# Cross-attention scores from the turned queries directly, recurrent scores on 32x64 pieces

## The chip, the cores and the metric

One core of a Trainium2 chip (trn2). The metric is device time in microseconds (us) for the whole program. TensorE (PE) multiplies; VectorE (DVE), ScalarE (ACT) and GpSimd (POOL) do elementwise work; SyncE (SP) issues every transfer. All engines share the on-chip memory (SBUF); PE writes to eight accumulation banks (PSUM).

## The reference, cut to what matters

A decoder layer for 32 sequences of 128 tokens, width 512, float32, in three residual blocks:

```python
x = x + recurrent(layernorm(x))      # 32 heads of 16
x = x + cross(layernorm(x), ctx)     # 32 query heads, 8 key/value heads of 16
x = x + ffn(layernorm(x))            # 512 -> 2048 -> 512, operands rounded in blocks of 32

# recurrent: r, k, v, g are projections of x mixed with its predecessor in time
att = rr @ kk * Wm                   # Wm: decay w^(t-s-1) for s < t, bonus u at s = t
y = att @ vv + rr @ state * wb       # chunks of 64 in the reference
# cross: 4 query heads share a key/value head; keys and values are both ctx
scores = einsum('bkgsd,bktd->bkgst', qh, kh) / sqrt(16)
out = einsum('bkgst,bktd->bkgsd', softmax(scores), vh)
```

Kernels here compute the recurrence for all 128 tokens at once, with a 128x128 decay table per head.

## The kernel before, in words

The 32 sequences are independent. Each engine has a block of code with small functions, one per step, with the sequence `n` as argument, and then a written-out list of calls: its program order. Semaphores named after the producer tie the engines. Lists for the first and last sequences are written out; the middle is a loop over `n` (10 to 28) with one period's calls, in which steps of up to five sequences are interleaved. Each engine works strictly through its list, so the place of a step in the list decides what waits behind it. SP has such a list too, and a transfer that waits for its source holds up all behind it.

On PE a period consists of, in this order before the change: `turn_x` (L496, transposes of the normalised x), `values_r` half 0 (L554), `turn_out` (L623), `scores_max` half 1 (L590), `project g`, `scores_max` half 0, `project r`, `scores_r` half 1 (L534), `turn_maxima` (L600), `project k`, `values_r` 1, `scores_x` 0 (L605), `head_variance` (L571), `project_v` (L515), `values_x` 0 (L612), `scores_x` 1, `up` 1 and 0 (L629), `project_out` (L578), `values_x` 1, `scores_r` 0, `down` 0 and 1 (L639), `turn_queries` (L584), `turn_sums` (L619), `up` 2 and 3. The four banks `rt` (one per row group g of the array) are shared by both kinds of scores and by the turned queries; `bank_o` holds transposes and outputs, `bank_a` and `bank_b` projections, `bank_y` the sums over values and `down`.

**Recurrent scores.** `scores_r(n, i)` does two of four blocks m of 128 channels. Row group g holds 32 channels, two heads of 16. The score of one head alone is had by setting the other head's 16 channels to 0 in one operand: POOL writes `rz` (late half of the receptances, two parities, L2947) and `kz` (early half of the keys, L2944) as products with a mask. Per m and g one matmul has all 128 keys against the late receptances of both parities (128 columns, L546) and one has the early keys of both parities against the early receptances (64 columns, L550). DVE multiplies with the decay table `wm` (`decayed`, L1451). `values_r` multiplies with the values: `vz` holds them spread with zeros, `vp` the early half of both parities stacked in partitions, which SP copies in two transfers (`earlier_values`, L216).

**Cross attention.** ACT writes the normalised x with the query heads reordered (`normalise_x`), PE turns it, ACT copies it as `qdense` (`queries_x`, L2396): 8 key/value heads x 16 channels in the partitions, then 4 query heads j and 128 tokens. `queries_spread` (L225) moves 16 partitions at a time so that each head of half i starts a 32-partition row group in `qx`: 4 transfers per half, 8 per sequence. `scores_max` (L590) computes the scores a first time, from `qx` and the turned context `kx`, 4 j x 4 g matmuls of 128 columns on 16 rows per half; DVE reduces them to the negated row maxima (`maxima`, L1484), PE turns these, ACT copies them, and `maxima_to_rows` (L245) puts them as a 17th row into `qx`. `scores_x` (L605) computes the scores a second time, transposed and with the maximum subtracted, 4 matmuls of 512 columns per half. ACT takes the exponential (`weights_x`), PE multiplies with the context (`values_x`), whose extra column of ones yields the sums. ACT copies the result (`out_x`, L2418), `outputs_gathered` (L235) moves the sums (1 transfer per half) and outputs (4 per half) to the dense layout for the turn back. DVE divides (`normalise_o`).

**Feed-forward.** `up` and `down` read bf16 operands that are rounded by chains on DVE (`hidden_*`, `gelu_*`) with one scaling per gelu half on POOL (`gelu_scale`, L2971), and turned by SP transfers (`hidden_turned` L259, `gelu_turned` L266). `first_sum` (DVE, L1477) follows `project_out`; the statistics of the next x and `normalise_q` (ACT) lead to `turn_x`.

## Time and profile before

| | us |
|---|---|
| median of 3 runs (lowest, highest) | 1427.66 (1426.7, 1431.09) |
| the profiled execution's own time | 1427.9 |
| its span in the profile | 1426.1 |
| PE busy (share), matmul records | 1285.7 (90%), 13352 |
| DVE busy (share) | 1137.4 (80%) |
| ACT busy (share) | 806.6 (57%) |
| POOL busy (share) | 657.5 (46%) |
| mean granted TensorE clock | 0.951 |

A float32 matmul appears as two records in the profile, so 16 matmuls are x32. In the timeline a group's length runs to the modelled end of its last matmul, which overlaps the next group; the time that a group takes from the engine is the distance of two starts. "Idle before" is the time the engine stood idle ahead of the group, with what ended it. The clock is given as a share of 2.4 GHz.

### The profile page before, as it was taken

To read this page: it belongs to the slowest core of one execution; us is meant where nothing else is said; L and a number is where in the kernel's file an instruction comes from. 1 tells how busy PE (TensorE), PEld (TensorE's weight loads), DVE (VectorE), ACT (ScalarE), POOL (GpSimd) and SP (SyncE) were. 2 spreads that over 40 slices of the span, in tenths; PEclk is the share of its full clock that TensorE was granted. 3 is DMA by queue.
4 is the path that set the end of the run, shared out by engine and by line. 5 is a ranking of instruction groups with operands and counts; after the bars stand their busy time and mean duration, and the time that the engine had idled before them with its cause. 6 is when DMAs were issued, how large, how long until landed. Compare 5 with 4: busy or idle time off the path is not lost.

```text
span 1426.1 us, 34930 instructions
## 1 busy us (share of the span) xinstructions
PE 1285.7 (90%) x13352; PEld 835.6 (59%) x13352; DVE 1137.4 (80%) x1960; ACT 806.6 (57%) x1541; POOL 657.5 (46%) x668
## 2 busy tenths in 40 slices
PE   2868789999999999999999999999999999999754
PEld 1745566556666665656666666656666666665321
DVE  5879778777878878888888878888887887877675
ACT  2233365656666656666666656656666665665441
POOL 3655445343545444544555454444455544543222
PEclk8878899999999999999999999999999999999776
DMA  9245313222212222222212222222221222222122
GB/s 307 56 121 126 71 41 60 64 58 52 61 45 59 56 61 57 66 64 52 62 46 57 54 66 57 66 64 63 54 62 42 63 54 64 57 66 57 36 49 48
DMA packets 143989, 95.04 MB, mean 67 GB/s; under 512 B 113744, under 2 KB 115792, under 8 KB 143056
## 3 DMA queue, kind: packets, MB, share of 16 engines
q1 hardware_dynamic: 143824, 92.80, 26.6%
q8 instruction: 108, 1.77, 0.5%
q14 instruction: 57, 0.47, 0.1%
HBM read 32.97 MB, written 8.39 MB: 29 GB/s over the span
## 4 chain that ended last, share of the span: by engine, by line
PE 74%; DVE 7%; DMA 6%; SPq 5%; issue 4%; ACT 2%; POOL 1%; POOLq 0%; DVEq 0%; ACTq 0%
PE bank_b L530 15%; PE bank_a L530 8%; PE bank_y L644 8%; PE bank_y L581 7%; PE bank_a L520 7%; PE rt L596 5%; PE rt L609 5%; PE bank_o L615 4%; DMA qx<-qdense 4%; SPq L233 3%; PE rt L546 3%; PE bank_o L575 2%; PE bank_b L635 2%; PE bank_a L635 2%; PE rt L550 1%
## 5 line engine op out<-in xcount | busy, mean ns | idle before, releaser
L2974 POOL TENSOR_TENSOR gmem<-gmem,unit_g 128x1024 bf16<-128x1024 bf16 x64 | 132.1, 2064 | 242.2 <-DVE unit_g L1540 242.2
L1488 DVE TENSOR_REDUCE negm<-rt 128x16 f32<-128x2048 f32 x64 | 146.4, 2287 | 44.2 <-PE rt L596 44.1
L2415 ACT ACTIVATE pT<-rt 128x2048 f32<-128x2048 f32 x64 | 120.1, 1877 | 45.2 <-PE rt L609 41.1
L644 PE MATMUL bank_y<-w2q,gmem 128*128 128x512 bf16 x512 | 123.4, 394 | 20.3 <-DMA gmem<-gmem 20.2
L530 PE MATMUL bank_b<-mix_k,w_Wk 128*128 128x128 f32 x1024 | 123.6, 280 | 15.4 <-DVE mix_k L1435 15.4
L530 PEld LDWEIGHTS bank_b<-mix_k,w_Wk 128*128 128x128 f32 x1024 | 121.9, 198 | 17.5 <-DVE mix_k L1435 12.8
L530 PE MATMUL bank_b<-mix_g,w_Wg 128*128 128x128 f32 x1024 | 130.8, 289 | 0.0
L530 PEld LDWEIGHTS bank_b<-mix_g,w_Wg 128*128 128x128 f32 x1024 | 125.1, 203 | 4.3 <-issue 0.7
L530 PE MATMUL bank_a<-mix_r,w_Wr 128*128 128x128 f32 x1024 | 126.7, 283 | 0.0
L530 PEld LDWEIGHTS bank_a<-mix_r,w_Wr 128*128 128x128 f32 x1024 | 120.7, 197 | 3.9 <-issue 0.4
L581 PE MATMUL bank_y<-w_Wo,yT 128*128 128x512 f32 x256 | 118.6, 607 | 3.6 <-DVE yT L1475 3.6
L2965 POOL TENSOR_TENSOR gt<-gt,yT 128x512 f32<-128x512 f32 x32 | 43.6, 1362 | 166.1 <-ACT yT L2394 166.0
L520 PE MATMUL bank_a<-w_Wv,mix_v 128*128 128x512 f32 x256 | 115.4, 593 | 3.3 <-ACT rT L2341 2.6
L1459 DVE TENSOR_TENSOR att<-rt,wm 128x1536 f32<-128x1536 f32 x64 | 112.0, 1749 | 4.9 <-PE rt L550 4.6
L2377 ACT ACTIVATE gh<-bank_b,all_columns 128x128 f32<-128x128 f32 x128 | 36.5, 369 | 126.5 <-PE bank_b L530 126.5
L596 PE MATMUL rt<-context,qx 16*128 16x128 f32 x2048 | 80.8, 297 | 28.0 <-DMA qx<-qdense 19.4
L644 PEld LDWEIGHTS bank_y<-w2q,gmem 128*128 128x128 bf16 x512 | 48.7, 100 | 82.2 <-issue 27.2
L596 PEld LDWEIGHTS rt<-context,qx 16*128 16x128 f32 x2048 | 68.9, 199 | 39.4 <-issue 27.3
L2958 POOL TENSOR_TENSOR gh<-gt,half_ln 128x512 f32<-128x512 f32 x32 | 53.9, 1684 | 77.6 <-DVE gt L1466 77.6
L520 PEld LDWEIGHTS bank_a<-w_Wv,mix_v 128*128 128x128 f32 x256 | 48.4, 190 | 64.2 <-issue 61.3
L2979 POOL TENSOR_TENSOR x<-x,o_bf 128x512 f32<-128x512 f32 x32 | 37.3, 1165 | 102.1 <-DVE o_bf L1607 102.1
L581 PEld LDWEIGHTS bank_y<-w_Wo,yT 128*128 128x128 f32 x256 | 49.2, 194 | 60.0 <-issue 56.3
(192 smaller groups left out, 2916.6 us busy)
## 6 DMA issues: line engine op xcount, KB each, us to landing
xin<-x SPq DMA_DIRECT2D x32, 256.0 KB, 3.0
gmem<-w SPq DMA_DIRECT2D x16, 512.0 KB, 4.0
vp<-vz SPq DMA_DIRECT2D x64, 128.0 KB, 2.9
context<-ctx SPq DMA_DIRECT2D x32, 256.0 KB, 2.7
qx<-qdense SPq DMA_DIRECT2D x256, 32.0 KB, 2.0
odense<-oT SPq DMA_DIRECT2D x256, 32.0 KB, 2.0
out<-x SPq DMA_DIRECT2D x32, 256.0 KB, 2.3
w_Wg<-Wg SPq DMA_DIRECT2D x1, 1024.0 KB, 7.6
```

What stands on the lines that cost most here:

```text
L520: done = e.matmul(bank_a[:, :], mix["v"][:, c, :], wt["Wv"][:, c, :], start=(c == 0), stop=(c == KT - 1))
L530: done = e.matmul(bank[:, m * T:(m + 1) * T], wt[f"W{name}"][:, c, m * P:(m + 1) * P], mix[name][:, c, :], start=(c == 0), stop=(c == KT - 1))
L581: done = e.matmul(bank_y[:, :], yT[:, c, :], wt["Wo"][:, c, :], start=(c == 0), stop=(c == KT - 1))
L596: done = e.matmul(rtb(g)[:, j * T:(j + 1) * T], qx[rows16, i, j, :], kx[n % 2][rows16, i, :], start=True, stop=True)
L609: done = e.matmul(rtb(g), kx[n % 2][rows32, i, :], qx[rows32, i, :, :], start=True, stop=True)
L615: done = e.matmul(bank_o[32 * g:32 * g + 32, :], kv[n % 2][:, 4 * i + g, :], pT[:, g, :], start=True, stop=True)
L635: done = e.matmul(bank[:, :], hqT[:, c, :], w1q[:, 4 * j:4 * j + 4, c, :], start=(c == 0), stop=(c == KT - 1))
L644: done = e.matmul(bank_y[:, :], gqT[:, t, :], w2q[:, t, :], start=(t == 0), stop=(t == FT - 1))
L1459: e.tensor_tensor(att[:, :, :, :, :].rearrange("p g m k t -> p g (m k t)"), rt[:, :].rearrange("p (g n) -> p g n", g=4)[:, :, 0:6 * HALF], ...
L1488: e.tensor_reduce(negm[:, 0:H].rearrange("p (g i j) -> p g i j", g=4, i=2)[:, :, i, :], rt[:, :].rearrange("p (g j s) -> p g j s", g=4, j= ...
L2415: e.activation(pT[:, :, :].rearrange("p g n -> p (g n)"), rt[:, :], ACT.Exp, scale=float(D) ** -0.5).then_inc(sem(f"act_ex{i}"), 1)
L2974: e.tensor_tensor(blocks(half), blocks(half), per_block(unit[f"g{i}"], 32), ALU.mult).then_inc(sem(f"pool_gsc{i}"), 1)
```

## The change

What it does:

- The turned context comes in a second form, `kd`: keys of two neighbouring heads in one row group, 256 columns, each with the other head's 16 rows at 0. `scores_max` multiplies `qdense` with it directly; half i now means query heads 2i and 2i+1 instead of key/value heads 4i to 4i+3. It waits for the ACT copy, no longer for a transfer.
- `queries_spread` is one step with two transfers of 112 partitions; `scores_x` and what follows take even key/value heads as half 0, odd ones as half 1. The even outputs are already in their place: ACT writes them to `odense`; the odd ones go through `oT` and four transfers.
- `kz` is gone. `rz` has four parts of 64 columns: early and late receptances of the first parity, late and early of the second. `scores_r` issues three matmuls per m and g (192, 128 and 64 columns) whose stationary side has 64 columns, two of them writing partitions 64 to 127.
- POOL fills `rz` in one step with three tensor_scalars. ACT copies the first parity of `vp`; one transfer is left.
- The order of the calls is new on all engines. The loop now covers n = 10 to 26.

Functions:

```diff
-ODD = 2 * H * D // 2 + D
+ODD = H * D + D
             def load_ctx(n):
...
+                        e.wait_ge(sem(f"pe_Xs{i}"), n - 1)
...
-            def queries_spread(n, i):
+            def queries_spread(n):
                 e.wait_ge(sem("act_qdense"), n + 1)
                 if n:
-                    e.wait_ge(sem(f"pe_Xt{i}"), n)
+                    e.wait_ge(sem("pe_Xt0"), n)
+                    e.wait_ge(sem("pe_Xt1"), n)
...
-                for g in range(4):
-                    kvh = 4 * i + g
-                    e.dma_start(qx[32 * g:32 * g + D, i, :, :], qdense[D * kvh:D * kvh + D, :, :])...
+                for i in range(2):
+                    e.dma_start(qx[0:P - D, i, :, :], qdense[D * i:P - D + D * i, :, :])...
+            def odd_outputs(n):
+                e.wait_ge(sem("act_oT1"), n + 1)
+                sums_gathered(n, 1, oT)
+                e.wait_ge(sem("sp_oden0"), 16 * (n + 1))
                 for g in range(4):
-                    kvh = 4 * i + g
-                    e.dma_start(odense[D * kvh:D * kvh + D, :, :], oT[32 * g:32 * g + D, i, :, :])...
+                    e.dma_start(odense[32 * g + D:32 * g + 32, :, :], oT[32 * g:32 * g + D, :, :])...
             def maxima_to_rows(n):
                 e.wait_ge(sem("act_neg"), n + 1)
+                e.wait_ge(sem("sp_qx"), 32 * (n + 1))
...
             def scores_r(n, i):
...
-                    for g in range(4):
-                        e.matmul(rtb(g)[:, mm * 3 * HALF:(mm * 3 + 2) * HALF], kT[rows32, m, :], rz[rows32, m, :, :], ...)
-                    for g in range(4):
-                        done = e.matmul(rtb(g)[:, (mm * 3 + 2) * HALF:(mm * 3 + 3) * HALF], kz[rows32, m, :, :],
-                                        rT[rows32, m, 0:HALF], ...)
+                pieces = ((0, 0, 0, 3), (1, 1, 1, 3), (1, 0, 3, 4))
+                    for side, keys, q0, q1 in pieces:
+                        for g in range(4):
+                            at = (3 * mm + q0 % 3) * HALF
+                            done = e.matmul(rtb(g)[HALF * side:HALF * side + HALF, at:at + (q1 - q0) * HALF],
+                                            kT[rows32, m, HALF * keys:HALF * keys + HALF], rz[rows32, m, q0:q1, :], ...)
             def scores_max(n, i):
                 e.wait_ge(sem(f"sp_ctx{n % 2}"), 16 * (n // 2 + 1))
-                e.wait_ge(sem(f"sp_qx{i}"), 64 * (n + 1))
-                for j in range(GQ):
+                e.wait_ge(sem("act_qdense"), n + 1)
+                for jj in range(2):
                     for g in range(4):
-                        done = e.matmul(rtb(g)[:, j * T:(j + 1) * T], qx[rows16, i, j, :], kx[n % 2][rows16, i, :], ...)
+                        done = e.matmul(rtb(g)[:, jj * 2 * T:(jj + 1) * 2 * T], qdense[rows32, 2 * i + jj, :],
+                                        kd[n % 2][rows32, :, :], ...)
...
+            def values_copied(n):
...
+                e.activation(vp[0:HALF, :, :], vz[0:HALF, 0:H * D].rearrange("p (q c) -> p q c", q=PAIRS), ACT.Copy)...
...
-            def earlier_keys(n):
-                of_parity(n, "pool_kz", kz, kT[:, :, 0:HALF], "act_kT")
-            def later_receptances(n):
-                of_parity(n, "pool_rz", rz, rT[:, :, HALF:T], "act_rT")
+            def by_parity(n):
+                e.wait_ge(sem("act_rT"), n + 1)
...
+                e.tensor_scalar(rz[:, :, 0:2, :], rT[:, :, :].rearrange("p k (e t) -> p k e t", e=2), parity[:, 0:1], 1.0, ...)
+                e.tensor_scalar(rz[:, :, 2, :], rT[:, :, HALF:T], parity[:, 1:2], 1.0, ALU.mult, ALU.mult)
+                e.tensor_scalar(rz[:, :, 3, :], rT[:, :, 0:HALF], parity[:, 1:2], 1.0, ...)
```

The orders of a period after the change, where they matter (each list goes round):

- PE: `head_variance`, `project_v`, `values_x` 0, `scores_x` 1, `up` 1, `up` 0, `project_out`, `scores_r` 0, `values_x` 1, `up` 2, `down` 0, `down` 1, `turn_queries`, `up` 3, `turn_sums`, `values_r` 0, `turn_x`, `scores_max` 1, `turn_out`, `project g`, `scores_max` 0, `project r`, `scores_r` 1, `turn_maxima`, `project k`, `values_r` 1, `scores_x` 0.
- ACT: ... `out_even`, `values_copied`, `weights_x` 1, two `gelu`, `out_odd`, `normalise_x`, `normalise_q`, `queries_x`, `x_turned`, `gate_tanh`, `gate_in`, two `gelu`, `maxima_turned`, `normalise_f`, `receptance`, `squares`. Before, `queries_x` came right ahead of `rstd_log q` and `normalise_q`.
- DVE: `norm_mv f` comes behind the second `maxima` and `mixed k` instead of ahead of them; `gelu_pow2` behind `gated_y`.
- POOL: `gate_rstd`, `by_parity`, `gelu_scale` 1, `gelu_scale` 0, `with_bias`, `last_sum`, `mixed r`, `second_sum`, `mixed g`, `gate_parts`. Before, `later_receptances` came ahead of `gate_rstd` and `earlier_keys` behind it.
- SP: `hidden_turned`, `even_sums`, `gelu_turned` 0, `earlier_values`, `gelu_turned` 1, `next_x`, `odd_outputs`, `load_ctx`, `queries_spread`, `store`, `maxima_to_rows`.
- At the start `Wv` is loaded ahead of the feed-forward weights, the third piece of these is loaded ahead of the first transposing transfer, and `project r` comes ahead of `project k` for sequence 0. At the end `up` of sequence 31 comes ahead of `down` half 1 of sequence 30, and on DVE the hidden state of 31 ahead of the last gelu half of 30.

## Rows read from the trace of the kernel before

**Rows 1.** The page, part 2: granted TensorE clock in the 40 slices.
```profile
PEclk8878899999999999999999999999999999999776
```

**Rows 2.** The page, part 4: the chain that ended last, by line.
```profile
PE bank_b L530 15%; PE bank_a L530 8%; PE bank_y L644 8%; PE bank_y L581 7%; PE bank_a L520 7%; PE rt L596 5%; PE rt L609 5%; PE bank_o L615 4%; DMA qx<-qdense 4%; SPq L233 3%; PE rt L546 3%; PE bank_o L575 2%; PE bank_b L635 2%; PE bank_a L635 2%; PE rt L550 1%
```

**Rows 3.** Stretches: us, busy (x) of PE, PEld, DVE, ACT, POOL, clock, DMA, GB/s.
```profile
251.20:1330.30 1079.10, 1041.80 (x11161) 678.16 (x11157) 877.38 (x1550) 672.79 (x1286) 511.59 (x529) 0.99 0.24 58
```

**Rows 4.** Waits of PE, 251.2 to 1330.3 us: total us, times, longest.
```profile
PE rt L596 <- DMA qx<-qdense: 15.2, 17, 2.0
PE bank_o L499 <- ACT xx L2316: 12.7, 26, 1.3
PE rt L596 <- DVE negm L1488: 3.4, 3, 1.8
```

**Rows 5.** Timeline of PE: start us, us, what, [idle before <-releaser].
```profile
974.80 1.12 PE L575 MATMUL bank_o<-yT,masks 128*128 128x512 f32 x2
...
1012.71 1.14 PE L609 MATMUL rt<-qx,context 32*128 32x512 f32 x8
1013.78 1.12 PE L575 MATMUL bank_o<-yT,masks 128*128 128x512 f32 x2
```

**Rows 6.** Timeline of PE in the same period, from project_out's end.
```profile
986.62 1.07 PE L615 MATMUL bank_o<-pT,context 128*32 128x512 f32 x8
987.62 0.50 PE L546 MATMUL rt<-rz,kT 32*128 32x128 f32 x8
...
988.67 3.63 PE L644 MATMUL bank_y<-w2q,gmem 128*128 128x512 bf16 x16
...
995.16 0.63 PE L499 MATMUL bank_o<-masks,xx 128*128 128x128 f32 x4 [0.42 <-ACT xx L2316]
995.72 0.32 PE L562 MATMUL bank_y<-att,vp 128*32 128x64 f32 x8
...
996.53 0.65 PE L626 MATMUL bank_o<-masks,odense 128*128 128x128 f32 x4
997.28 1.17 PE L596 MATMUL rt<-context,qx 16*128 16x128 f32 x32
998.38 3.84 PE L530 MATMUL bank_b<-mix_g,w_Wg 128*128 128x128 f32 x32
```

**Rows 7.** Timeline of PE at 517 us, and the stretch 518 to 524 us.
```profile
517.13 1.77 PE L596 MATMUL rt<-context,qx 16*128 16x128 f32 x32 [1.67 <-DMA qx<-qdense]
518.84 6.46 PE L530 MATMUL bank_b<-mix_g,w_Wg 128*128 128x128 f32 x32
...
518.00:524.00 6.00, 6.00 (x43) 5.78 (x37) 3.62 (x5) 0.00 (x0) 2.69 (x3) 0.50 0.05 11
```

**Rows 8.** Timelines of ACT and of SP's queue in that period.
```profile
992.77 0.60 ACT L2401 ACTIVATE qdense<-rt 128x512 f32<-128x512 f32 x1 [1.31 <-PE rt L587]
...
993.39 2.40 SPq L233 DMA_DIRECT2D qx<-qdense  x4
```

**Rows 9.** Timelines of POOL, at the start and in that period, and of DVE.
```profile
42.67 3.02 POOL L2924 TENSOR_SCALAR mix_g<-xx,all_columns 128x128 f32<-128x128 f32 x4
...
979.48 1.04 POOL L2939 TENSOR_TENSOR kz<-kT,masks 128x512 f32<-128x512 f32 x1
981.19 2.27 POOL L2974 TENSOR_TENSOR gmem<-gmem,unit_g 128x1024 bf16<-128x1024 bf16 x1 [0.68 <-DVE unit_g L1540]
...
983.90 0.41 DVE L1587 TENSOR_SCALAR gmem<-gmem 128x1024 f16<-128x1024 bf16 x1
...
986.73 0.69 DVE L1482 TENSOR_TENSOR x<-bank_y,xin 128x512 f32<-128x512 f32 x1 [0.55 <-PE bank_y L581]
```

**Rows 10.** SP's queue, PE's first up, and the median landing from the issues by line.
```profile
978.42 1.26 SPq L264 DMA_TRANSPOSE hqT<-hz  x1
...
981.36 1.04 PE L635 MATMUL bank_b<-w1q,hqT 128*128 128x512 bf16 x4
...
hqT<-hz SPq DMA_TRANSPOSE x32, 2.5
```

More of the change, by code:

```diff
@@ new lines, in _ @@
+            e.wait_ge(sem("act_expv"), 51)
+            values_x(24, 0)
+            e.wait_ge(sem("act_ex0"), 25)
+            scores_x(24, 1)
+            e.wait_ge(sem("act_kT"), 27)
+            up(23, 1, bank_b)
+            e.wait_ge(sem("dve_vz"), 27)
+            up(23, 0, bank_a)
+            e.wait_ge(sem("dve_yz"), 26)
+            project_out(25)
+            e.wait_ge(sem("act_ex1"), 25)
+            scores_r(26, 0)
+            e.wait_ge(sem("act_oT0"), 25)
+            values_x(24, 1)
@@ new lines, in _ @@
+            scores_x(25, 1)
+            e.wait_ge(sem("act_kT"), 28)
+            up(24, 1, bank_b)
+            e.wait_ge(sem("dve_vz"), 28)
+            up(24, 0, bank_a)
+            e.wait_ge(sem("dve_yz"), 27)
+            project_out(26)
+            e.wait_ge(sem("act_oT0"), 26)
+            values_x(25, 1)
+            e.wait_ge(sem("act_ex1"), 26)
+            scores_r(27, 0)
+            e.wait_ge(sem("dve_ze0"), 25)
+            up(24, 2, bank_a)
+            e.wait_ge(sem("dve_x1"), 27)
@@ new lines, in _ @@
+                gelu_quantised(n - 4, 0)
+                decayed(n - 1, 1)
+                stats_g(n - 3)
+                norm_mv("g", n - 3)
+                mixed(n, "v")
+                weighted(n - 3)
+            hidden(23)
+            hidden_max(23)
+            hidden_pow2(23)
+            hidden_scale(23)
+            hidden_round(23)
+            hidden_quantised(23)
+            gelu_max(22, 1)
+            scaled_y(25)
+            spread_v(26)
+            gated_y(25)
+            gelu_pow2(22, 1)
@@ new lines, in _ @@
+            up_out(23, 1, bank_b)
+            up_out(23, 0, bank_a)
+            gelu_round(22, 1)
+            gelu_quantised(22, 1)
+            first_sum(25)
+            stats_x(25)
+            norm_mv("x", 25)
+            gelu_max(23, 0)
+            gelu_pow2(23, 0)
+            decayed(26, 0)
+            stats_q(27)
+            norm_mv("q", 27)
+            second_out(22)
+            residual(22)
+            denominators(24)
+            up_out(23, 2, bank_a)
+            up_out(23, 3, bank_b)
@@ new lines, in _ @@
+            gelu_round(23, 0)
+            differences(27)
+            maxima(25, 1)
+            normalise_o(24)
+            stats_f(24)
+            maxima(25, 0)
+            norm_mv("f", 24)
+            mixed(27, "k")
+            gate(26)
+            gelu_quantised(23, 0)
+            decayed(26, 1)
+            stats_g(24)
+            norm_mv("g", 24)
+            mixed(27, "v")
+            weighted(24)
+            hidden(24)
+            hidden_max(24)
+            hidden_pow2(24)
@@ L3226 @@
     pairs = np.arange(H).reshape(2, 2, 4, 2).transpose(0, 2, 1, 3).reshape(PAIRS, 2)
[L3227 removed]
+    order = np.stack([np.concatenate([pairs[:, a:a + 1], pairs], 1).reshape(3 * PAIRS) for a in range(2)])
     heads = np.concatenate([get("L0_attn_time_decay")[order], get("L0_attn_time_faaaa")[order]], 1)
```

1744 lines of the change are left out of this document (983 added, 761 removed).

## The prediction

> **What bounds the kernel now.** I read the slices of the page first, then the chain, then three stretches, then one period. In the slices [rows 1] the granted TensorE clock is full (9 of 10 or more) from the sixth slice to the last few. In the chain that ended last [rows 2] every costly entry is a PE line, with two exceptions that belong together: the transfer of the queries (4%) and its issue on SP's queue (3%). So TensorE's instruction order is the path, and the spread of the queries is the one thing outside it that the path passes through often. The stretches [rows 3] cut the run where it changes character: 251.2 us of start, 1079.1 us in the middle, 95.7 us of end. The middle begins and ends with the same instruction (the head variance) 27 sequences apart, so a period is 1079.1/27 = 39.97 us. PE is busy 1041.8 of it: 37.3 us are idle, and three rows hold 31.3 of them [rows 4]: 15.2 for the queries' transfer, 12.7 for the normalised x, 3.4 for the row maxima. A period without trouble takes 1013.78 - 974.80 = 38.98 us [rows 5]. Beside the idle time there is a hidden loss: behind a wait of 1.67 us for the queries, the projection of g took 6.46 us instead of 3.84 and the clock stood at 0.50, the 1.2 GHz level, for 6 us [rows 6, 7]. Four such drops stand in the middle, each right behind such a wait; the others are shorter, and I count 2.1 us each, 8.5 us. DVE (877.4 of 1079.1) is the next engine, with 19% to spare.
>
> **Queries.** Today scores_max waits until four transfers per half have landed: the copy of the turned queries takes 0.60 us, the issue of one half 2.40 us, and then the landing follows [rows 8]. After the change it waits for the ScalarE copy alone. The 15.2 us and the 8.5 us of clock go. The new transfers (two of 112 rows, then the maxima) are needed only by scores_x, more than 10 us later, so their size (by the code 0.46 MB for the pair against 0.26) costs nothing unless they hold up the maxima behind them, for whose transfer PE waits nowhere in the middle today [rows 4]. SP issues 16 instead of 27 transfers a period. Outputs: the even half is copied straight into its place; four transfers instead of eight, none of which PE waited for in the middle. Gain 0, cover kept. The context load grows by half and is issued over one period ahead.
>
> **What is late next.** In ScalarE's order the copy of the queries moves behind normalise_q, which shortens the chain to turn_x by about 0.5 us (0.60 less overlap); on PE the first values_r (996.53 - 995.72 = 0.81 us) moves ahead of turn_x. From the end of project_out (986.62) to turn_x (995.16) are 8.54 us, of which 0.42 is the wait [rows 6]. The chain behind it then needs 8.0, while PE has 8.9 us of work: the wait goes, 12.7 us. The copy of the queries then ends about 0.6 us before PE asks for it. The maxima: scores_max for half 1 moves ahead of turn_out (997.28 - 996.53 = 0.75 us more for the reduction), so 3.4 us go too.
>
> **First scores.** Before, each half was 16 matmuls of 128 columns on 16 rows, 998.38 - 997.28 = 1.10 us. After, 8 of 256 columns on 32 rows. Per row group both stream 512 columns; scores_x, 4 matmuls of 512, takes 1013.78 - 1012.71 = 1.07 [rows 5, 6]. Bounds 1.07 and 1.20 (were the wider load exposed); I take 1.07, saving 0.06 per period.
>
> **Recurrent scores.** Before: 988.67 - 987.62 = 1.05 us per half for 384 columns per row group [rows 6]. After: 12 matmuls per m, in two column halves of the array with 192 columns each, loads of 64 instead of 128 columns. scores_x and values_r (384 columns in 0.81) both run at 2.1 ns per column. If the halves run side by side, that is 384 x 2.1 = 0.81 us; if they take turns, 768 x 2.1 = 1.61. The nearest row is values_r, many short matmuls on parts of the array that do overlap, but there no piece follows another on the same row group with other columns. I take 1.00, a fifth over the floor: 0.05 saved twice, 0.10 per period. The first range end saves 0.48, the last costs 1.12.
> The Trainium skill (TensorE: Matmul & The Clock Gate, Part 3, "The mechanism") says that weight loads overlap running matmuls only when the row group differs. By it the loads of the second column half would wait for the first half's streams, which is the second rival below. Its page TensorEngine Tiling (Array Packing), "Key Properties", says that different tiles load and multiply in parallel, which is the low end. No row of the kernel before has two column pieces in one row group, so the trace does not decide.
>
> **Other engines.** POOL: two products of 512 elements, 1.04 us each [rows 9], become three tensor_scalars with 1024 elements in all. Two products' worth is 2.1 us; eight of the 128-column tensor_scalars are 6.0 us at the worst row (four in 3.02, beside DVE, at the start). I take 2.5. What queues behind it is the scale of the gelu half (starts 981.19, 2.27 us), for which DVE's rounding waits (starts 983.90). It would start about 982.0 and end 984.3: DVE's rounding 0.4 us late, inside the 0.55 us that DVE idles before first_sum. Cost 0. ACT gets the copy of the first values: 64 rows of 512 at most the 0.60 us of the queries' copy; it stands ahead of weights_x(1), whose result is not needed for 3 us. ACT is busy 672.8 of 1079.1. Cost 0. DVE: norm_mv f moves behind the maxima, 0.3 us onto the chain to the turned hidden states. That transfer is issued at 978.42, lands 2.5 us later at 980.9, and up begins at 981.36 [rows 10]: 0.4 us of slack, of which 0.3 go by this and 0.05 by faster scores. I leave 0.1 us per period for it and for the transfers whose issue now and then takes a microsecond longer.
>
> **The sum.** Middle, per period: 39.97 - 0.56 (queries) - 0.31 (clock) - 0.47 (turn_x) - 0.13 (maxima) - 0.16 (scores) + 0.10 = 38.44, so -1.53, times 27 = -41 us. Start, 6 sequences: the same, less because other waits set their end, -1.0 each, -6. There Wv is also loaded earlier, and the third piece of W1 before the transposes; I count nothing for it but 8 us in the range. End, 2 sequences: -3, and hidden(31) now runs ahead of the last gelu half, -2. Together -52. The profiled execution took 1427.9 us (span 1426.1), 0.2 over the median of 1427.66, so the two need no correction: 1427.7 - 52 = 1375.5; I say 1375.
>
> **The rivals.**
> 1. *A new wait keeps the period near the untroubled one.* The chain through DVE (maxima, mixing, gate, decayed scores, hidden states, transposing transfer) has 0.4 us of slack and gets longer while PE gets shorter. For it: DVE would be at 33/38.4. Against: in the period of [rows 5] PE waits for nothing but x. It would hold 39.1 us: gain 0.87 x 27 = 23, plus 11: 1393.
> 2. *The column halves take turns*, or the loads are exposed: 1.61 instead of 1.00 per half, +1.2 us per period in all 32, +38: 1413. For: the scores of today, 1.05 against a floor of 0.81, already show loads [rows 6]; against: values_r at its floor.
> 3. *Slower.* POOL's parity step is the mechanism. Its output is ready far ahead of scores_r, but the gelu scale queues behind it, and behind that DVE's rounding, first_sum, the statistics, turn_x. The chain has 0.5 us (DVE's idle time) and 0.9 us (PE's slack at turn_x). At 2.5 us nothing happens; each microsecond over about 3.5 is one per period; from about 5.4 us on, the 52 us are lost. At the 6.0 us of the worst row: 2.5 x 27 = 67 lost, 1442. For: [rows 9], 3.02 for four. Against: in the same place today nothing contends, 1.04 for 512.
> 4. *The change takes nothing off the path*: another transfer of that place in SP's queue (the outputs, the maxima) inherits the long issue and lands just as late for PE. Then only scores and turn_x gain, 0.5 x 32 = 16 from the 52 remain, 1412; with the scores at their high bound, no change at all. Against: in the middle PE waited for none of them once.
>
> **Numbers.** Chances: forecast 0.60, first rival 0.14, second 0.11, fourth with some gain 0.05, no change 0.03, slower 0.07. All pieces at their floor (-0.38 x 32 = -12), the start 8 better and the end 4 better give 1351 at the low end; at the high end the range takes in rivals 1, 2 and 4: 1413. A difference under 0.3% (4 us) could not be told from none. Faster 0.90, same 0.03, slower 0.07.
>
> **What would show it.** Right: no wait of PE for the queries' transfer; full clock in the middle; head variances 38.2 to 38.7 us apart; scores_r 0.9 to 1.1 us per half; turn_x without its 0.42. Wrong: a wait of up for hqT in each period (rival 1); recurrent scores near 1.6 us (2); a parity step over 3.5 us and DVE waiting for the gelu scale (3); PE waiting for odense or the maxima's row (4).

## The result and the profile after

The changed kernel takes 1364.58 us (median of 4 runs, 1364.28 to 1369.35), the kernel before in the same comparison 1429.38 us (1426.7 to 1432.94). The ratio is 0.9553, with a 95% interval of 0.9521 to 0.9585: about 64 us faster, where 52 were forecast. The profiled span is 1362.5 us. In the chain of the changed kernel TensorE's share is 80%, and DMA's is 3% over all its transfers; before, the queries' transfer and its issue alone held 7% [rows 2].

The page of the changed kernel, parts 1 and 2 (busy time with its share and instructions; granted TensorE clock in 40 slices):

```profile
PE 1254.7 (92%) x13352; PEld 801.5 (59%) x13352; DVE 1137.3 (83%) x1960; ACT 823.8 (60%) x1577; POOL 631.8 (46%) x700
...
PEclk8878899999999999999999999999999999999876
```

The same three stretches as before, cut at the same two head variances (us, then busy time and instructions of PE, PEld, DVE, ACT, POOL, then clock, DMA share, GB/s):

```profile
0.00:247.50 247.50, 180.56 (x1964) 128.41 (x1964) 198.93 (x302) 107.31 (x216) 119.69 (x129) 0.89 0.41 113
247.50:1275.60 1028.10, 1022.12 (x11168) 654.54 (x11164) 879.37 (x1553) 682.43 (x1314) 488.92 (x557) 1.00 0.26 63
1275.60:1362.50 86.90, 52.00 (x229) 18.56 (x225) 58.99 (x108) 34.03 (x47) 23.17 (x14) 0.76 0.22 50
```

Against [rows 3] the middle lost 1079.1 - 1028.1 = 51.0 us, the start 251.2 - 247.5 = 3.7, the end 95.8 - 86.9 = 8.9. In the middle TensorE is idle for 6.0 us where it was idle for 37.3, and its clock is 1.00 where it was 0.99. The waits over 0.2 us that are left there (total us, times, longest) come once each; neither the queries' transfer nor the normalised x of [rows 4] is among them:

```profile
PE rt L566 <- DVE negm L1614: 1.6, 1, 1.6
PE bank_y L580 <- DVE att L1585: 1.6, 1, 1.6
PE bank_o L516 <- DVE x L1630: 1.5, 1, 1.5
PE bank_b L654 <- DMA hqT<-hz: 0.8, 1, 0.8
```

The periods are 38.04 us in all but a few of the 27, and in such a period TensorE waits for nothing. This is the one that answers to [rows 5, 6], on PE's timeline:

```profile
973.89 1.12 PE L593 MATMUL bank_o<-yT,masks 128*128 128x512 f32 x2
...
985.71 1.14 PE L566 MATMUL rt<-rz,kT 32*64 32x192 f32 x48
986.78 1.07 PE L633 MATMUL bank_o<-pT,context 128*32 128x512 f32 x8
...
993.50 0.24 PE L640 MATMUL bank_o<-masks,oden 32*128 32x32 f32 x1
993.67 0.32 PE L580 MATMUL bank_y<-att,vp 128*32 128x64 f32 x8
...
994.48 0.66 PE L516 MATMUL bank_o<-masks,xx 128*128 128x128 f32 x4
995.07 1.15 PE L614 MATMUL rt<-context,qdense 32*128 32x256 f32 x16
996.14 0.66 PE L645 MATMUL bank_o<-masks,odense 128*128 128x128 f32 x4
996.63 3.74 PE L547 MATMUL bank_b<-mix_g,w_Wg 128*128 128x128 f32 x32
...
1011.93 0.70 PE L593 MATMUL bank_o<-yT,masks 128*128 128x512 f32 x1
```

Read it from start to start, since the printed durations overlap. The first scores take 996.14 - 995.07 = 1.07 us. The recurrent scores take 986.78 - 985.71 = 1.07, where they took 1.05: the pieces of 32x64 gave nothing. The turning of the outputs takes 0.49 us, where it took 0.75 [rows 6], of which TensorE idled for 0.09. The input is turned at 994.48 with no wait.

POOL's parity step in that period:

```profile
978.47 0.69 POOL L3251 TENSOR_SCALAR rz<-rT,masks 128x512 f32<-128x512 f32 x1
979.13 0.48 POOL L3253 TENSOR_SCALAR rz<-rT,masks 128x256 f32<-128x256 f32 x1
979.58 0.48 POOL L3254 TENSOR_SCALAR rz<-rT,masks 128x256 f32<-128x256 f32 x1
981.09 1.90 POOL L3282 TENSOR_TENSOR gmem<-gmem,unit_g 128x1024 bf16<-128x1024 bf16 x1 [1.02 <-DVE unit_g L1667]
```

SP's queue, the issue of the hidden states' transfer:

```profile
976.89 1.23 SPq L273 DMA_TRANSPOSE hqT<-hz  x1
```

The parity step takes 1.6 us (2.5 forecast), and POOL then waits 1.02 us for DVE. `up` starts at 980.45, 3.56 us after that issue, which leaves 1.1 us over the 2.5 of [rows 10]; the forecast had counted on 0.1.

### The profile page after: what moved, and what is told of

The parts are those of the page before. It is cut to its first block, busy times and chain, and to the rows that moved or that the text cites. A ratio compares the mean times of both kernels' runs of the same rounds, so it can differ in the third digit from the quotient of the medians.

```text
span 1362.5 us, 34643 instructions
## 1 busy us (share of the span) xinstructions
PE 1254.7 (92%) x13352; PEld 801.5 (59%) x13352; DVE 1137.3 (83%) x1960; ACT 823.8 (60%) x1577; POOL 631.8 (46%) x700
## 4 chain that ended last, share of the span: by engine, by line
PE 80%; DVE 8%; issue 5%; DMA 3%; POOL 2%; ACT 2%; POOLq 0%; SPq 0%; DVEq 0%; ACTq 0%
PE bank_b L547 15%; PE bank_a L547 8%; PE bank_y L599 8%; PE bank_y L663 7%; PE bank_a L537 7%; PE rt L614 5%; PE rt L566 4%; PE rt L627 4%; PE bank_o L633 4%; PE bank_b L654 4%; PE bank_a L654 4%; PE bank_o L593 2%; PE bank_y L585 2%; PE bank_y L580 1%; DMA gmem<-w 1%
## 5 line engine op out<-in xcount | busy, mean ns | idle before, releaser
L3282 POOL TENSOR_TENSOR gmem<-gmem,unit_g 128x1024 bf16<-128x1024 bf16 x64 | 124.5, 1945 | 239.1 <-DVE unit_g L1667 239.1
L2626 ACT ACTIVATE pT<-rt 128x2048 f32<-128x2048 f32 x64 | 120.1, 1876 | 20.2 <-PE rt L627 19.4
L547 PE MATMUL bank_b<-mix_g,w_Wg 128*128 128x128 f32 x1024 | 120.6, 276 | 0.0
L547 PEld LDWEIGHTS bank_b<-mix_g,w_Wg 128*128 128x128 f32 x1024 | 117.2, 192 | 1.6 <-issue 1.3
L2578 ACT ACTIVATE gt<-bank_b,half_bg 128x128 f32<-128x128 f32 x128 | 36.6, 370 | 83.3 <-PE bank_b L547 83.3
L566 PEld LDWEIGHTS rt<-rz,kT 32*64 32x64 f32 x3072 | 63.1, 131 | 33.3 <-issue 24.0
L1655 DVE TENSOR_REDUCE amax_g<-gmem 128x32 f32<-128x1024 bf16 x64 | 77.8, 1215 | 1.7 <-ACT gmem L2658 1.6
L1719 DVE SCALAR_TENSOR_TENSOR gmem<-gmem,pow_g 128x1024 bf16<-128x1024 f16 x64 | 78.2, 1222 | 1.1
```

The lines of the kernel that those rows point to most:

```text
L547: done = e.matmul(bank[:, m * T:(m + 1) * T], wt[f"W{name}"][:, c, m * P:(m + 1) * P], mix[name][:, c, :], start=(c == 0), stop=(c == KT - 1))
L566: done = e.matmul(rtb(g)[HALF * side:HALF * side + HALF, at:at + (q1 - q0) * HALF], kT[rows32, m, HALF * keys:HALF * keys + HALF], rz[rows ...
L1655: e.tensor_reduce(amax[key][:, :], blocks(src), AX_X, ALU.max, apply_absolute_value=True).then_inc(sem(name), 1)
L1719: e.scalar_tensor_tensor(blocks(half), blocks(half.bitcast(FP16)), MAGIC16, per_block(pow2[f"g{i}"], 32), ALU.subtract, ALU.mult).then_inc ...
L2626: e.activation(pT[:, :, :].rearrange("p g n -> p (g n)"), rt[:, :], ACT.Exp, scale=float(D) ** -0.5).then_inc(sem(f"act_ex{i}"), 1)
L3282: e.tensor_tensor(blocks(half), blocks(half), per_block(unit[f"g{i}"], 32), ALU.mult).then_inc(sem(f"pool_gsc{i}"), 1)
```

## Experiments

Times "in place of" are against the changed kernel's 1364.58 us and ratio of 0.9553. "The middle" is always from the fifth to the last head variance, 27 periods.

**1. The old recurrent scores in the changed kernel.**

```
-  pieces = ((0, 0, 0, 3), (1, 1, 1, 3), (1, 0, 3, 4))
+  e.matmul(rtb(g)[:, (mm * 3 + 1) * HALF:(mm * 3 + 3) * HALF], kT[rows32, m, :], rz[rows32, m, :, :],
+           start=True, stop=True)
+  e.matmul(rtb(g)[:, mm * 3 * HALF:(mm * 3 + 1) * HALF], kz[rows32, m, :, :], rT[rows32, m, 0:HALF],
+           start=True, stop=True)
```

> The changed kernel with the recurrent scores of the kernel before (a 128-column and a 64-column matmul for each head on 32x128 pieces, the keys' parity product back on POOL); order of the work and cross attention as changed. Theory: the 32x64 pieces gave nothing (scores_r takes 1.07 us in the changed kernel, 1.05 before), so 1364 us, 1360 to 1368. Rival, as forecast: the pieces save 0.05 us per half, two halves in 32 batches, so 3 us slower, 1368. Second rival: the 0.41 us per period of the middle that no wait explains came from the pieces, so 27 x 0.41 = 11 us slower, 1376.

Measured: 1364.99 us, ratio 0.9562 (0.9539 to 0.9585), the same. The undisturbed period is 38.00 us, 0.04 shorter than with the pieces. PE's timeline shows the half as it was before:

```profile
757.42 0.50 PE L565 MATMUL rt<-rz,kT 32*128 32x128 f32 x8
...
758.20 0.35 PE L569 MATMUL rt<-rT,kz 32*128 32x64 f32 x8
758.47 0.64 PE L635 MATMUL bank_o<-pT,context 128*32 128x512 f32 x4
```

1.05 us, from 757.42 to 758.47. By time alone the first rival's 3 us could not be told from nothing; the period can: by that rival it would be 38.14 us. So the third part of the change is worth nothing, both rivals fall, and the gain is in the other two parts.

**2. The wait for the queries' transfers put back.**

```
 def scores_max(n, i):
     e.wait_ge(sem("act_qdense"), n + 1)
+    if 8 <= n <= 24:
+        e.wait_ge(sem("sp_qx"), 32 * (n + 1))
```

> The changed kernel in which the first scores of batches 8 to 24 also wait for the two transfers of queries that they no longer read. Theory: these transfers were the bound. They are issued at 994.10 in the traced period, take 2.13 us of issuing and some 3.1 to land, so they are back at about 998.3, and the first scores, which start at 995.07, lose 3.2 us in each of 17 periods: 55 us, and some 5 more for clock drops, so 1420 us (1405 to 1435); TensorE's waits on qx come back. Rival: other work slides into the gap (the first scores' place was not what bound), under 10 us, 1374 at most.

Measured: 1448.12 us, ratio 1.0128 (1.0089 to 1.0167): 84 us more than the changed kernel, and 0.9 to 1.7% more than the kernel before, above the range that was given. PE's waits, 400 to 1200 us; then one of them on PE's timeline; then the stretch behind it:

```profile
PE rt L616 <- DMA qx<-qdense: 52.3, 17, 3.6
```

```profile
725.86 2.09 PE L616 MATMUL rt<-context,qdense 32*128 32x256 f32 x16 [3.10 <-DMA qx<-qdense]
727.88 1.11 PE L647 MATMUL bank_o<-masks,odense 128*128 128x128 f32 x4
728.79 5.19 PE L547 MATMUL bank_b<-mix_g,w_Wg 128*128 128x128 f32 x32
```

```profile
725.86:733.96 8.10, 8.10 (x56) 7.23 (x56) 3.58 (x3) 0.00 (x0) 2.31 (x2) 0.63 0.00 1
```

The wait came out as worked out, 52.3 us over 17 periods against 54. The clock did not: 5 us were allowed for it, and some 30 are there: the middle grew by 1112.8 - 1028.1 = 84.7 us, of which the wait is 52.3. Behind a wait of 3.10 us the granted clock is 0.63 for the next 8.1 us, and the same projection takes 5.19 us in place of 3.74. At 15 of the 17 waits the clock falls to half, during the wait or just behind it, for 71 us in all. So a wait of the first scores for this transfer is paid in full and more, and in the new order it would be worse than it was in the old one (3.1 us each, against 15.2 us in 17 waits).

**3. The new data flow alone**, in the order of the kernel before and with its recurrent scores: `scores_max` reads `qdense` against `kd`, two transfers for the queries, four for the outputs and two for the sums; SP's list has the queries as one step in place of two, and nothing else is changed.

> The kernel before with the changed data flow of cross attention alone (first scores from the turned queries against a dense copy of the keys, four transfers for queries and for outputs); its order of the work and its recurrent scores stay. Theory: the data flow takes away the wait for the queries (15.2 us of the middle) and the clock drops (8.5), and the order gave the rest, so 24 us less than 1429, 1405 (1398 to 1412). Rival A: the order was worth nothing by itself, and this kernel has nearly the whole gain, 1375 or less. Rival B: in the old order the next wait (the turned input's, 12.7 us in the middle, or the maxima's) grows by what the queries' loses, and the time is above 1418.

Measured: 1391.44 us, ratio 0.9739 (0.9714 to 0.9765). That is 36 us of the gain, 12 more than the theory gave; rivals A and B fall. The stretches (three, as above) and PE's waits in the middle:

```profile
0.00:244.80 244.80, 179.36 (x1803) 126.76 (x1804) 200.79 (x301) 102.57 (x209) 122.92 (x125) 0.90 0.44 119
244.80:1297.40 1052.60, 1024.03 (x10268) 653.05 (x10293) 876.94 (x1550) 673.17 (x1286) 512.40 (x529) 1.00 0.25 64
1297.40:1389.80 92.40, 53.67 (x229) 19.15 (x233) 61.63 (x111) 31.41 (x47) 22.73 (x14) 0.78 0.22 51
```

```profile
PE bank_o L494 <- ACT xx L2313: 12.8, 26, 1.3
PE rt L591 <- DVE negm L1484: 6.2, 8, 1.8
```

Of the 36 us, 26.5 are in the middle: the queries' 15.2, the clock's 8.5, and an undisturbed period that is 38.76 in place of 38.98 us (27 x 0.22 = 5.9), less 2.8 by which the wait for the maxima grew (26.8 together). The wait for the normalised x is what it was, 12.8 us in 26 periods. So the order of the work is what takes it away, and the order is worth the other 24.5 us of the middle (1052.6 - 1028.1). By the rows that is nearly this wait's 12.8, 4.6 of the maxima's (6.2 to 1.6), and 8.1 from shorter steps in an undisturbed period (27 x 0.30, its wait of 0.42 left out). Whether the order costs something in the start is not shown: it is 244.8 us here and 247.5 in the changed kernel, but in the nine runs whose order of the start is the changed kernel's (it and runs 1, 2, 4 to 7, 11 and 12) it lies between 244.2 and 248.8.

**4 to 6. Which step of the order.** Both moves around the turning of the input undone in the 17 periods of the loop, then each alone.

```
 # TensorE (runs 4 and 5)             # ScalarE (runs 4 and 6)
-values_r(n - 1, 0)                   +queries_x(n - 2)
 turn_x(n)                             rstd_log("q", n); rstd_exp("q", n); normalise_q(n)
+values_r(n - 1, 0)                   -queries_x(n - 2)
```

> The changed kernel in which, in the 17 periods of the loop, TensorE's turning of the next input stands ahead of the first half of the recurrent values again, and ACT's copy of the queries ahead of the logarithm for the next input. Theory: turning the input waits 0.4 us again, since the chain from project_out to it is 7.9 us long and TensorE has that much less between them, so 17 x 0.45 = 8 us slower, 1372 (1368 to 1376). Rival: the wait is made up later in the period, within 2 us of 1364.

Measured: 1386.03 us, ratio 0.9707 (0.9685 to 0.9728): 21 us more, not 8. Each of the 17 periods is 39.48 us, 1.44 over 38.04. ACT's timeline, then PE's:

```profile
776.54 0.60 ACT L2612 ACTIVATE qdense<-rt 128x512 f32<-128x512 f32 x1 [1.15 <-PE rt L605]
777.04 0.28 ACT L2510 ACTIVATE logv_q<-mv_q,eps 128x1 f32<-128x1 f32 x1
```

```profile
778.93 0.63 PE L516 MATMUL bank_o<-masks,xx 128*128 128x128 f32 x4 [1.39 <-ACT xx L2529]
```

ACT waits 1.15 us for TensorE's turned queries, with the logarithm for the next input queued behind; in the changed kernel that logarithm needed only 0.23 us of waiting for DVE. The copy's 0.5 us and the wait's 1.15, less those 0.23, are the 1.4 us by which the normalised x is later. The run isn't the old order again, in which only 0.42 us were waited: there TensorE turned the queries 17.3 us behind the head variance (992.13 - 974.80), and here as in the changed kernel 18.2 us behind it (992.11 - 973.89), since one `up` now stands ahead of it. With the copy back in its old place, the normalised x therefore comes at 21.1 us and not at 20.2 as in the kernel before.

> As the run with both orders put back, but TensorE's order alone is put back (turning the next input ahead of the first half of the recurrent values); ACT keeps the changed order. Theory from that run's trace: the 1.44 us per period came from ACT, where the copy of the queries waits 1.15 us for TensorE's turning and the logarithm for the next input stands behind it. With ACT's order as changed the normalised input is there 19.7 us into the period and the old place of the turn begins at 19.8, so nothing is lost: 1364.5 us (1362 to 1368). Rival, as forecast: TensorE's order carries the gain, 17 x 0.4 us = 7 us slower, 1371.

Measured: 1372.65 us, ratio 0.9609 (0.9580 to 0.9639), period 38.56 (+0.52). The theory said +0 and fell, but not in favour of the rival's reason either: the normalised x is there, and the turn waits for something that no text had named (7.7 us in 17 waits).

```profile
768.24 0.24 PE L640 MATMUL bank_o<-masks,oden 32*128 32x32 f32 x1
768.93 0.66 PE L516 MATMUL bank_o<-masks,xx 128*128 128x128 f32 x4 [0.45 <-DVE rden L1622]
```

The input is turned into `bank_o`, into which the sums were turned just before, and DVE must take their reciprocals out of it first. The values, which use another bank, fill that round trip.

> The other half of that run: ACT's order alone is put back (copy of the queries ahead of the logarithm), TensorE keeps the changed order. Theory: the input is ready 1.5 us later, at 21.2 us into the period, and TensorE, which comes to its turn at 20.6 with the values already done, waits 0.65 us in each of 17 periods: 11 us slower, 1375.5 (1372 to 1379); so values ahead of the turn are worth 0.8 us per period, but only with the late ACT. Rival: the whole 1.44 us stays, 1386 as in the run with both.

Measured: 1372.80 us, ratio 0.9608 (0.9583 to 0.9633), period 38.67 (+0.63), within the range of the theory; the waits for xx sum to 10.0 us in 17 periods. The three runs fit one rule: the turn starts at the last of three times, counted from the head variance. The sums' reciprocals are out of the bank at 20.3 us, the normalised x is there at 19.7 with the new order on ACT and at 21.1 with the old one, and with the values ahead TensorE itself comes at 20.6. Either move alone leaves half a microsecond, both are needed, and undoing both costs more (1.44) than the two single costs together (1.15), because the 0.81 us of values then stand behind the wait and no longer fill it.

**7. A longer parity step on POOL**, the forecast's rival on the slow side.

```
 def by_parity(n):
+    e.tensor_tensor(spare2, rT, rT, ALU.mult)
+    e.tensor_scalar(spare[:, :, 0:2, :], rT[:, :, :].rearrange("p k (e t) -> p k e t", e=2), parity[:, 0:1], 1.0, ALU.mult, ALU.mult)
+    e.tensor_scalar(spare[:, :, 2, :], rT[:, :, HALF:T], parity[:, 1:2], 1.0, ALU.mult, ALU.mult)
+    e.tensor_scalar(spare[:, :, 3, :], rT[:, :, 0:HALF], parity[:, 1:2], 1.0, ALU.mult, ALU.mult)
```

> The changed kernel in which POOL's parity step also multiplies into a spare buffer (the same three products once more, and a product of the receptance with itself), so that it takes about 4.4 us in place of 1.6. Theory from the changed kernel's trace: POOL waited 1.02 us for DVE behind this step, so the scaling of the gelu blocks starts 1.8 us later; DVE's 1.11 us of idle time ahead of the first sum takes most of it, and TensorE's 0.85 us between the normalised input and its turn the rest: nothing is lost, 1364.5 us (1362 to 1370). Rival, as in the forecast's third rival: the cover ends at 3.5 us and each us beyond costs one, 0.9 us in 32 periods, 1393 us. If the transposing transfers of the gelu, which stand behind the same scaling, have no slack, the wait shows at TensorE's down product.

Measured: 1379.28 us, ratio 0.9657 (0.9629 to 0.9686), 15 us more. From the first to the last of its instructions the step took 4.6 us (median), where it took 1.6. PE's waits in the middle:

```profile
PE bank_b L656 <- DMA hqT<-hz: 6.9, 6, 1.2
PE rt L568 <- DVE negm L1616: 4.6, 6, 1.6
PE rt L568 <- POOL rz L3261: 2.4, 2, 1.4
```

DVE's timeline, in the changed kernel and then in run 7:

```profile
985.82 0.69 DVE L1608 TENSOR_TENSOR x<-bank_y,xin 128x512 f32<-128x512 f32 x1 [1.11 <-PE bank_y L599]
```

```profile
766.34 0.43 DVE L1716 TENSOR_SCALAR gmem<-gmem 128x1024 f16<-128x1024 bf16 x1 [1.20 <-POOL gmem L3289]
```

Neither theory holds. DVE now idles ahead of the rounding, for POOL's scaling, and no longer ahead of the first sum (0.03 us there on average, where it was 1.04). That much is the forecast's chain. Its end is another: TensorE waits only 0.2 us for the normalised x in all of the middle, and instead for the row maxima and the hidden states' transfer. That these come late because everything behind the first sum slips on DVE fits the rows, but no run takes it apart. Twice TensorE waits for the parity step's own output, which the forecast had called ready far ahead. The forecast's rule (free up to 3.5 us, then one for one) gives 1.1 us per period at 4.6, and 0.57 were paid (middle 1043.5 us). If each further microsecond costs one, the cost starts near 4 us; one point can't tell that from a slower rise. At the 1.6 us that the step really takes there is none.

**8 to 10. The head of the program.** The start gained less than forecast. In the changed kernel TensorE's first projection starts at 42.34 us, because DVE's statistics of the first input stand behind the scaling of a weight block whose load lands at 31.3:

```profile
31.30 1.22 DVE L1739 TENSOR_REDUCE amax_w<-gmem 128x32 f32<-128x1024 f32 x1 [4.86 <-DMA gmem<-w]
...
32.95 0.69 DVE L1521 BATCH_NORM_STATS2 stats_q<-xin 128x6 f32<-128x512 f32 x1
```

Run 8 moves the first input ahead on DVE, ACT and POOL and loads Wr first; run 9 also moves the first values' bias, the second input's differences and the first decays ahead of weight blocks; run 10 also the first batch's gated output and the third input's load. DVE's order in run 10, in the part that changed (the statistics of the first input stand ahead of `distances`):

```
 w12_scale(0); w12_scale(1); w12_quantise(0)
+differences(0); bonus_added(0); w12_quantise(1); mixed(0, "k"); bonus_added(1); mixed(0, "v")
+stats_q(1); w12_scale(2); w12_quantise(2); spread_v(0); w12_scale(3); differences(1)
+w12_quantise(3); decayed(0, 0); w12_scale(4); mixed(1, "k"); w12_scale(5); decayed(0, 1)
+w12_quantise(4); gate(0); w12_quantise(5); w12_scale(6); scaled_y(0); gated_y(0)
```

> The changed kernel with another head: the statistics and the normalising of the first input ahead of the building of the decays, its differences and mixes ahead of the scaling of the third block of weights, and Wr loaded first among the four projection weights. Theory: TensorE's first projection starts at 42.3 us now, since DVE's statistics stand behind the scaling of a block of weights that lands at 31.3; here it starts at 27 to 30, and the start to batch 4 gets 5 to 12 us shorter: 1355 us (1352 to 1360). Rival: the scaling and turning of the feed-forward weights set the pace of the start by themselves, the lead is given back before batch 4, and the time stays within 3 us of 1364.5.

Measured: 1360.96 us, ratio 0.9534 (0.9507 to 0.9561).

> The run with the early first input, and in it also DVE's bias of the first values, the second input's differences and the first decays moved ahead of the scaling of weight blocks, with POOL's and SP's queues to match. Theory: in that run TensorE had its first three products done at 39.6 us and then waited 14.6 us for the second input, because DVE's 0.7 us of work on the first values stood behind the weight blocks until 52; here that wait is 2 to 4 us, and the start to batch 4 gets 6 to 10 us shorter, 1353 us (1349 to 1357). Rival: DVE's and POOL's total work on the sixteen blocks sets the pace, and the lead is lost at batches 1 to 3 as before: 1359 to 1362.

Measured: 1358.09 us, ratio 0.9515 (0.9489 to 0.9541).

> The run with the early values, and in it also DVE's two steps on the gated output of the first batch, the second batch's mix for the values and POOL's parity step of it moved ahead of the scaling of the sixth to eighth weight blocks; the load of the third input stands ahead of the tenth block's. Theory: in that run TensorE waited 12.2 us at the first output projection because these steps stood behind weight blocks until 73.4 us; they can be done at 66, and 4 to 7 us of it reach batch 4, 1352.5 us (1349 to 1356). Rival: the sixteen blocks set the pace, and what is won at batch 0 is waited for at batches 1 to 3, 1356 to 1360.

Measured: 1355.25 us, ratio 0.9505 (0.9488 to 0.9523). The waits on PE's timeline at the head, run 8, run 9 and run 10:

```profile
25.96 6.61 PE L547 MATMUL bank_a<-mix_r,w_Wr 128*128 128x128 f32 x32 [9.01 <-POOL mix_r L3242]
...
54.16 1.08 PE L516 MATMUL bank_o<-masks,xx 128*128 128x128 f32 x4 [14.59 <-ACT xx L2530]
```

```profile
42.62 1.00 PE L516 MATMUL bank_o<-masks,xx 128*128 128x128 f32 x4 [2.42 <-ACT xx L2530]
...
73.60 5.29 PE L599 MATMUL bank_y<-w_Wo,yT 128*128 128x512 f32 x8 [12.17 <-DVE yT L1601]
```

```profile
66.62 5.50 PE L599 MATMUL bank_y<-w_Wo,yT 128*128 128x512 f32 x8 [5.83 <-DVE yT L1601]
```

Each run removes the wait that it aims at, and most of what it wins is waited for at the next place. The first projection starts 16.4 us earlier in run 8 and the fifth head variance only 2 (245.5 against 247.5 us), which is within the 244.2 to 248.8 of the other runs; it is at 242.0 in run 9 and at 237.3 in run 10, where the first head variance is 14.6 us early (59.7 against 74.3). Part of the lead is also paid to the clock: the projection that starts at 25.96, behind 9.01 us of idling, takes 6.61 us at a mean granted clock of 0.55, where an undisturbed one takes 3.74 to 3.84 at full clock. Neither theory nor rival holds whole: the weight blocks do not set the pace by themselves, but every step that is moved ahead finds one behind it that wasn't. Only run 10 came out within the range given for it. The intervals of runs 8 and 9 overlap that of the changed kernel. Run 10 is by the ratios 0.5%, some 7 us, faster than the changed kernel, with intervals that just touch (0.9488 to 0.9523 and 0.9521 to 0.9585), so it is probably the fastest here; its middle is the same 1028.1 us, and the start is 10.2 us shorter (1.0 of it stands at the very start, where Wv lands at 8.1 in place of 9.1 us).

**11 and 12. Why the pieces gave nothing.** Run 11 leaves the scores of the first keys against the last 64 query columns out.

Its edit is the first added line, run 12's the second:

```
-pieces = ((0, 0, 0, 3), (1, 1, 1, 3), (1, 0, 3, 4))
+pieces = ((0, 0, 0, 3), (1, 1, 1, 3))
+pieces = ((0, 0, 0, 3), (1, 0, 3, 4), (1, 1, 1, 3))
```

> The changed kernel without the third of the three pieces of the recurrent scores (first keys against the last 64 query columns), which leaves out that part of the scores. Theory: the first two pieces do run side by side (in the trace the 128-column piece starts 25 ns after the 192-column one on the same rows), and the 1.07 us per half comes from the third, which stands behind the second on the same columns of the array and holds up the next four heads in TensorE's order: a half takes 0.80 to 0.90 us here, 0.2 us less, 1364.5 - 32 x 0.4 = 1352 us (1349 to 1357). Rival: the 192-column pieces or the loads set the time, a half stays at 1.00 to 1.07, and the time is within 4 us of 1364.5.

> The changed kernel with the pieces in the order 192, 64, 128 columns in place of 192, 128, 64. Theory: the short piece is done while the 192 columns stream, and the second one of its array columns follows without holding up the next heads: 0.95 to 1.02 us per half in place of 1.07, 2 to 6 us less, 1361 us (1358 to 1364). Rival: the order within a column half makes no difference, since both orders stream 192 columns there: 1.07 us, 1364.5 within 3.

Measured: run 11 1358.16 us, ratio 0.9502 (0.9479 to 0.9526), 1 us above its range, though the half takes what its theory said; run 12 1364.67 us, ratio 0.9549 (0.9531 to 0.9568), the same as the changed kernel. PE's timeline, run 11, then run 12:

```profile
756.24 0.88 PE L566 MATMUL rt<-rz,kT 32*64 32x192 f32 x32
757.05 0.64 PE L633 MATMUL bank_o<-pT,context 128*32 128x512 f32 x4
```

```profile
756.78 1.14 PE L566 MATMUL rt<-rz,kT 32*64 32x192 f32 x48
757.86 0.64 PE L633 MATMUL bank_o<-pT,context 128*32 128x512 f32 x4
```

Two pieces take 757.05 - 756.24 = 0.81 us. That is the forecast's floor for 384 columns at 2.1 ns each, with the 128-column pieces wholly hidden: one behind the other, the 640 columns of a row group would take 1.34 us at that rate (an estimate). So the two column halves do work side by side. The third piece, of 64 columns, adds 0.26 us, and it adds as much when it comes second (1.08), so the theory of run 12 (a blocked order) falls. What the third piece pays for (its loads, its place in TensorE's queue, or the change of columns) stays open; its share of the columns alone isn't it, since its half of the array then streams 192 columns like the other. Run 11 also shows what is late next. Its undisturbed period is 37.52 us, and the hidden states' transfer is waited for again:

```profile
PE bank_b L654 <- DMA hqT<-hz: 8.2, 7, 1.4
```

## Why the prediction was right, and where not

- **Direction, mechanism, range.** Right: 1364.6 lies within 1351 to 1413, 10 us under the 1375. The middle gained 51.0 us where 41 were forecast. What had been said would show it right is there: no wait for the queries' transfer, full clock in the middle, turn_x without its wait. The head variances are 38.04 us apart, below the 38.2 to 38.7 that were given.
- **Queries, 15.2 us of wait.** Right, by runs 2 and 3. The larger transfers cost nothing in the middle, where TensorE never waits for them or for the maxima behind them.
- **Clock, 8.5 us.** Right in kind: the middle's clock is 1.00, also in run 3, and run 2 brings the drops back. The 8.5 us are half of the 17 us that the clock stood at 0.50 in four drops. A fifth, from 1319.7 us on, fills the last 10.6 us of the middle before, behind a wait of 1.82 us for the row maxima; the forecast rightly kept it out, and the changed kernel has one in that place too, 4.5 us of it in the middle. The price of such drops is not a fixed addition to each wait: run 2's text allowed 5 us for them and some 30 came.
- **turn_x, 12.7 us.** Right that the wait goes, by both moves together. The chain from project_out's end to the normalised x was put at 8.0 us and is 993.59 - 985.71 = 7.9, with TensorE coming at 8.8 (8.9 forecast). The reason for the move on TensorE was incomplete: by itself it covers DVE's reciprocals (run 5).
- **Maxima, 3.4 us.** 1.6 are left, in one wait; a term of 0.13 per period was 0.07.
- **First scores.** 1.07 us, as taken.
- **Recurrent scores: the term that failed.** 1.00 us was taken per half, 1.07 came, so the 0.10 gained per period was 0.04 lost (run 1). The halves do overlap, which the range's low end had supposed and the rule of the Trainium skill, "TensorE: Matmul & The Clock Gate", Part 3, "The mechanism", speaks against (weight loads overlap only when the row group differs). If the loads of the second half had waited for the first half's streams, run 11 would be well over its 0.81 us; the trace disagrees with the rule, or the rule does not mean pieces in other columns. "TensorEngine Tiling (Array Packing)", "Key Properties" (different tiles load and multiply in parallel) in the Trainium skill agrees with run 11 and doesn't explain the 0.26 us of the third piece.
- **Allowance of 0.10 for the hidden states' transfer.** Not needed: 0.8 us in all of the middle, slack 1.1 us and not 0.1. It was worked out from DVE's move of norm_mv f alone, and the transfer is issued 3.00 us after the head variance, where it was 3.62 [rows 5, 10].
- **The unforecast part, 0.5 us per period.** This is where the forecast was short. An untroubled period was put at 38.98 - 0.42 - 0.16 + 0.10 = 38.50, and is 38.04, although the recurrent scores gave 0.14 less than taken and only the 0.10 of allowance came back. So 0.50 us came from elsewhere, 13.5 us in 27 periods. Counted from start to start it is small items: turning the outputs 0.75 to 0.49 (0.09 of it idling before), the projection of g behind it 3.77 to 3.67, turning the queries 0.53 to 0.44, the `up` halves 0.08 together, less 0.03 for turning the input. They change when their neighbours are others; why, no run shows. Run 3 has 0.22 of the change from 38.98 with the new data flow alone (turning the outputs 0.59), the rest comes with the order. The forecast moved these steps without asking what follows them. Without these 13.5 us the time would be 1378 us, an estimate: that the 1375 is so near is in part good luck, since the recurrent scores' miss of 3.8 us and others pull the other way.
- **Start and end.** -3.7 for -6 and -8.9 for -5. The start differs by 4.6 us between runs with the same order of it, so the 2.3 us of the miss say nothing. What can be won there lies in the place of the weight blocks in the queues: with steps moved ahead of them the first output begins 14.6 us earlier (run 10). The end is 3.4 us shorter in run 3 and 8.9 with the order.
- **Rivals.** The new wait on the hidden states (1) isn't there at 38.0 us and is at 37.5 (run 11). Taking turns (2) is refuted by the 0.81 us of run 11. The parity step (3) costs something at 4.6 us, by another wait than the one named, and nothing at 1.6 (run 7). An inheriting transfer (4) isn't there: PE waits in the middle for one transfer, once (the hidden states', 0.8 us).

## What to carry to other kernels

Ask of each transfer on the path whether its reader could take the data as they lie: here the spread of the queries was needed by the later product only, and its price was the wait (15.2 us) plus the slow clock behind it (8.5). When an order written out by hand is changed, list for the moved instruction every time that can hold it (its operand, its bank's last reader, its own engine), and move against the latest; undoing one of two such moves tells less than undoing both. Splitting matmuls onto smaller parts of the array is worth measuring piece by piece: here a second piece beside the first was free and a third one took back all that the split had won.

## What the runs showed of the hardware that was not expected

- Two column halves of one row group work at the same time in float32: 192 and 128 columns per row group, twice, take 0.81 us, what 2 x 192 take at the 2.1 ns per column of the other float32 steps (run 11). A third piece of 64 columns on one of the halves costs 0.26 us in either order (run 12, and the changed kernel).
- A wait of 3.1 us in otherwise full work is followed by 8.1 us at a mean granted clock of 0.63, so for most of it at the 1.2 GHz level; over 17 waits that is some 30 us beside 52 of waiting (run 2). It doesn't come each time: at 15 of the 17 waits of 2.8 to 3.6 us in run 2, behind four of the 17 for the queries in the kernel before (those of 1.16, 1.34, 1.67 and 1.68 us, but not the longest, of 1.98), and behind none of the 17 of 1.4 us in run 4.
- A turning of four 128x128 blocks takes 0.49 us from start to start ahead of a projection (changed kernel), 0.59 ahead of the first scores (run 3), and 0.66 with 0.09 of idling behind it in the kernel before.
